# A graph kernel whose edge scores are scattered earlier, with the diagonal written by SyncE

## The reference

```
xl = (x @ Wl).reshape(n, H, D);  xr = (x @ Wr).reshape(n, H, D)      # H = 4 heads of 64
msg = xl[src] + xr[dst]
act = jnp.where(msg > 0, msg, 0.2 * msg)
e = jnp.einsum('ehd,hd->eh', act, att)       # one number per edge and head
m = segment_max(e, dst);  p = exp(e - m[dst]);  alpha = p / denom[dst]
```

## Time and profile before

| | |
|---|---|
| median of 3 runs (lowest to highest) | 3180.23 us (3179.59 to 3190.14) |
| the profiled execution: time, span | 3187.83 us, 3186.1 us |
| busy: TensorE, VectorE, ScalarE, GpSimd | 87%, 51%, 30%, 25% of the span |
| TensorE clock granted, mean | 0.906 of full speed |
| front, count | 0 to 93 us, 93 to 370 us |
| mix 0, output 0 | 370 to 934 us, 934 to 1076 us |

### The profile page before, as it was taken

How to read it: one execution, slowest core, us unless ns; L and a number is a source line. 1 busy time by engine, 2 the same in 40 slices (tenths; PEclk the granted TensorE clock), 3 DMA queues, 4 the chain that set the end, 5 groups by cost and what they waited for, 6 DMA issues and landing times. The chain is left out here.

```text
span 3186.1 us, 52553 instructions
## 1 busy us (share of the span) xinstructions
PE 2769.6 (87%) x19788; PEld 2590.7 (81%) x19788; DVE 1615.7 (51%) x3224; ACT 963.7 (30%) x1941; POOL 791.7 (25%) x780
## 2 busy tenths in 40 slices
PE   6577798988879699879997999899999989999478
PEld 6344587877879699778886999899999989999367
DVE  7466455555566288665555222245454432226455
ACT  4355322322231155314443000034333220001043
POOL 0456555554654133212210000000000001000144
PEclk9788798888889799859998999999999999999589
DMA  8733322323236698227765211111111662124174
GB/s 244 251 84 98 92 77 78 80 83 86 59 122 179 155 229 213 94 71 199 207 178 125 79 44 44 56 30 54 31 57 54 184 163 86 60 68 135 27 239 141
DMA packets 206775, 363.00 MB, mean 114 GB/s; under 512 B 38358, under 2 KB 139950, under 8 KB 205299
## 3 DMA queue, kind: packets, MB, share of 16 engines
q1 hardware_dynamic: 170117, 278.93, 30.2%
q0 software_dynamic: 36432, 80.98, 10.1%
HBM read 272.99 MB, written 98.18 MB: 116 GB/s over the span
## 5 line engine op out<-in xcount | busy, mean ns | idle before, releaser
L180 PE MATMUL mix_bank<-mix_wkv_hi,layer_act_hi 128*125 128x256 f32 x1280 | 368.2, 288 | 12.4 <-issue 12.0
L182 PE MATMUL mix_bank<-mix_wkv_hi,layer_act_lo 128*125 128x256 f32 x1280 | 366.5, 286 | 12.4 <-issue 12.1
L181 PE MATMUL mix_bank<-mix_wkv_lo,layer_act_hi 128*125 128x256 f32 x1280 | 366.7, 286 | 10.9 <-issue 10.3
L3084 POOL TENSOR_TENSOR sage_add<-sage_add,sage_bias 125x256 f32<-125x256 f32 x40 | 29.6, 742 | 1205.5 <-DMA sage_add<-resid 1205.5
L180 PEld LDWEIGHTS mix_bank<-mix_wkv_hi,layer_act_hi 128*125 128x125 f32 x1280 | 244.0, 191 | 22.2 <-issue 21.9
L567 POOL DMA_INDIRECT scored_ring<-xl,edge_idx x168 | 171.6, 1021 | 348.3 <-DVE edge_e L651 218.7
L181 PEld LDWEIGHTS mix_bank<-mix_wkv_lo,layer_act_hi 128*125 128x125 f32 x1280 | 244.5, 191 | 13.7 <-issue 13.2
L182 PEld LDWEIGHTS mix_bank<-mix_wkv_hi,layer_act_lo 128*125 128x125 f32 x1280 | 244.2, 191 | 12.9 <-issue 12.7
L924 PE MATMUL count_pa<-count_hot_s,count_hot_d 125*125 125x416 bf16 (+1 forms) x624 | 156.3, 417 | 68.2 <-DVE count_hot_s L834 36.0
L574 POOL DMA_INDIRECT scores<-edge_e,edge_idx x168 | 174.4, 1038 | 133.2 <-DMA scores<-edge_e,edge_idx 86.3
L924 PEld LDWEIGHTS count_pa<-count_hot_s,count_hot_d 125*125 125x125 bf16 x624 | 101.6, 169 | 123.2 <-DVE count_hot_s L834 49.0
(11 more groups left out here) (596 smaller groups left out, 8325.5 us busy)
## 6 DMA issues: line engine op xcount, KB each, us to landing
ffn_raw<-in_L_ffn_w_dram SPq DMA_DIRECT2D x16, 2048.0 KB
scores<-targets_hole SPq DMA_DIRECT2D x40, 546.9 KB
ffn_raw<-in_L_ffn_W_dram SPq DMA_DIRECT2D x16, 1024.0 KB
gat_sc<-scores SPq DMA_DIRECT2D x6, 2187.5 KB
mix_raw<-in_L_mix_w_qkv_dram SPq DMA_DIRECT2D x24, 512.0 KB
scored_ring<-scores SPq DMA_DIRECT2D x4, 2187.5 KB
layer_slab<-in_L_gnn_W_neigh_dram SPq DMA_DIRECT2D x7, 1024.0 KB
layer_slab<-in_L_gnn_W_self_dram SPq DMA_DIRECT2D x7, 1024.0 KB
```

The lines of the kernel that those rows point to most:

```text
L180: pe.matmul(out, lhs[0], rhs[0], start=first, stop=False)
L181: pe.matmul(out, lhs[0], rhs[1], start=False, stop=False)
L182: return pe.matmul(out, lhs[1], rhs[0], start=False, stop=last)
L3084: pool.tensor_tensor(add[:, u % 2, :], add[:, u % 2, :], bb[:, g * SLAB:(g + 1) * SLAB], ALU.add) \
```

## The change

The lag is 2 batches from the first scatter to the last; SyncE writes the diagonal, right behind its last fill, under a semaphore of its own; GpSimd's first scatter waits for that. In count the first turn is followed by 4 steps in place of 2 and the last by 1 in place of 3. In output 0 one step stands ahead of the first remainder in place of two, the next ones ahead of k = 2, 4, 6 in place of 1, 4, 7, and the last ones come later (the last in tile 7 of slab 2, not in tile 1). The number of gathers, scatters and steps is the same.

```
-LAG = 8
-CATCH = 6
+BEHIND = 2
+AT_ONCE = 2
...
     def scatter(self, pool, b, j):
...
-        pool.wait_ge(self.s_sc, 16 * (T + 1) + 16 * k)
+        if k == 0:
+            pool.wait_ge(self.s_diag, 16 * (T + 1))
+        else:
+            pool.wait_ge(self.s_sc, 16 * k)
...
-    def diagonal(self, pool):
-        pool.wait_ge(self.fill.s_fill, self.fill.count)
+    def diagonal(self, sp):
+        sp.wait_ge(self.fill.s_fill, self.fill.count)
...
     def gpsimd(self, pool, first, end):
...
         for b in range(first, end):
-            done = range(self.written(b - 1) if b else 0, self.written(b))
-            if 0 in done:
-                self.diagonal(pool)
             for j in range(EB):
                 if b + AHEAD < BATCHES:
                     self.gather(pool, b + AHEAD, j)
-                for d in done[:1]:
-                    self.scatter(pool, d, j)
-            for d in done[1:]:
-                for j in range(EB):
-                    self.scatter(pool, d, j)
+                if b >= BEHIND:
+                    self.scatter(pool, b - BEHIND, j)
...
                 counts.fill.issue(sp, len(counts.fill.left))
+                edges.diagonal(sp)
...
-                    while todo.u < COUNT_BATCHES * (t + 1) // T:
+                    while todo.u < min(COUNT_BATCHES, AT_ONCE + COUNT_BATCHES * (t + 1) // T):
...
-                for _ in range(2):
-                    if todo is not None:
-                        todo.step()
+                if todo is not None:
+                    todo.step()
                 for k in range(KD):
-                    if todo is not None and k in (1, 4, 7):
+                    if todo is not None and k in (2, 4, 6):
...
-                        if todo is not None and i in ((5, 9), (1, 4, 6, 9), (1, 4, 6, 9), (2, 5, 8))[g] and todo.left():
+                        if todo is not None and i in ((5, 9), (1, 4, 7), (1, 4, 7), ())[g] and todo.left():
```

More of the change, by code:

```diff
@@ L526, in __init__ @@
         self.s_idx, self.s_att, self.s_cell = ph.sem("idx"), ph.sem("att"), ph.sem("cell")
-        self.s_e, self.s_sc = ph.sem("e"), ph.sem("sc")
+        self.s_e, self.s_sc, self.s_diag = ph.sem("e"), ph.sem("sc"), ph.sem("diag")
         self.s_g, self.s_link = ph.sems("g", RING), ph.sem("link")
@@ L581, in diagonal @@
             n = min(R, N - 1 - t * R)
[L582 to L587, removed]
+            sp.dma_start(diag[t * R:t * R + n, 0:HEADS], self.loops[0:n, t, :]).then_inc(self.s_diag, 16)
+        sp.dma_start(self.scores[N * N - 1:N * N, :], self.loops[R - 1:R, T - 1, :]).then_inc(self.s_diag, 16)
     def landed(self, eng):
-        eng.wait_ge(self.s_sc, 16 * (T + 1) + 16 * ET)
+        eng.wait_ge(self.s_sc, 16 * ET)
     def gpsimd(self, pool, first, end):
@@ L604, in gpsimd @@
                     self.gather(pool, b + AHEAD, j)
-                for d in done[:1]:
-                    self.scatter(pool, d, j)
-            for d in done[1:]:
-                for j in range(EB):
-                    self.scatter(pool, d, j)
+                if b >= BEHIND:
+                    self.scatter(pool, b - BEHIND, j)
         if end == BATCHES:
-            for d in range(self.written(end - 1), end):
+            for d in range(end - BEHIND, end):
                 for j in range(EB):
```

## The result

The changed kernel takes 3227.4 us (median of 4 runs, 3215 to 3245) against 3180.6 (median of 4) before. By the medians it is 47 us slower, and outside the range of 3167 to 3195. The profiled execution took 3244.7 us, 17 above its median, so its rows overstate the loss a little (span 3243.0 against 3186.1: +56.9).

The account below looks back on a forecast made before the run. Bounds: VectorE-TensorE ring in count, TensorE slowed by late instructions in mix 0, VectorE's first remainder at output 0's start. Terms +3.0 + 4 - 5 - 0.8 = +1.2 us on 3187.8 gave 3189.0, median 3181.4; range 3167 to 3195.

Parts of the forecast that it names:

- Twelve scatters more in count: Count stage, turns 2 and 3: the extra early scatters lengthen turns by +4 us, between 0 and 11.4.
- the long burst stalls the counting loops: Rival, turns 2 and 3: GpSimd issuing without pause from 157 to 215 us costs +13.6, 3194 us; chance 0.15.
- Nobody waits: Count: gathers of batches 7 and 8 held behind GpSimd's waiting scatter delay nobody; VectorE needs batch 8 after turn 2; cost 0.
- Two steps more after turn 0: Count, before turn 1: two more VectorE steps of 2.26 us each cost +1.3 to +4.5 us, taken as +3.0.
- Mix 0: -5: Mix 0: fewer GpSimd issues, in catch-up batches and the first 25 us, save 5 us; bounds -1.5 to -10.
- Instructions come late while requests are under way: Mix 0: TensorE's slabs take 70.7 us against 49.85 in mix 1 because instructions arrive late during GpSimd's gathers and scatters.
- Two steps fewer after turn 9: End of count: VectorE's work ends earlier, but the stage ends with SyncE's store, so 0.
- the diagonal on SyncE: Count: SyncE issues the diagonal by 155 us, ahead of its store at 159.84; cost 0.
- the last scatters: End of output 0: 14 gaps of 4.0 us end at 1065.2, before the last store at 1074.35; cost 0.
- Output 0: -0.8: Output 0, first slab: remainder ends 2.26 us earlier, TensorE waits 1.3 for the seventh; gain 0.8, bounds 0 to -2.3.
- turn 1 after 146: Count: turn 1's first one-hot tile was expected at 142 to 145 us; after 146 would mean late gathers.
- turns 2 and 3 above 27 and 25: Count: turns of 24 and 20 us would mean no burst price; 27 and 25 would point to the burst rival.

## Why the prediction was wrong

- *Twelve scatters more in count: +4, at most 11.4.* This step failed. The mechanism is the one of the rival "the long burst stalls the counting loops", in its place (turns 2 and 3), to which I gave 0.15. The early scatters alone lengthen these turns by 11.2 us in one profile; that this is nearly the rival's 11.4 is luck, for with the moved output steps beside them (which cost nothing by themselves) it is 16, and with the count steps 28 and 31 (two profiles of the changed kernel). The price had been taken from turn 4 of before, and a turn that lies almost wholly beside requests has no row in that trace, so the nearest row was no upper bound. As a whole the early scatters cost 29.5 us, so about 18 lie outside these turns; the profiles point to mix 0, and their cause is open. "Nobody waits" for the gathers behind the diagonal was true for their data and false for what their issue does to the others.
- *Two steps more after turn 0: +3.0, at most 4.5.* Also failed in its size: 1.0053, 17 us (9 to 25). Their own 4.5 us are there (turn 1 starts 6.5 later). The rest goes with the gathers that they release, 16 in a row, which no run takes away by themselves, and with the later place of the diagonal and the first scatters. I had counted what the steps issue on VectorE and not what they set free on GpSimd. The two parts, 1.0093 and 1.0053, add up to 1.0146; the whole is at 1.0122 and 1.0132.
- *Mix 0: -5.* This step failed too, in its sign as far as can be told. Mix 0 was 10 us longer in the profile; between its first and last key/value unit it was 528.8 us against 525.0. One program's mix 0 on this kind was 550 and 566 us in two profiles, so a term of 5 can't be seen in a pair, but the seven profiles with the short lag are 18 us longer on average than the five with the old one. The mean price was about right: (565.6 - 421.3) / 313 requests is 0.46 each, where I had worked out 0.43. The 25 requests fewer (288 in the trace; I had counted 23 fewer) did not bring that price back: a mean price is no price of one request more or less.
- *Instructions come late while requests are under way:* right in what sets off the waits. The kernel that leaves the requests out shows 52.7 us a slab against 70.7, close to the slab of mix 1, on the same kind of chip. That it is the supply of instructions which is late is inferred from waits with no name; no row shows it.
- *Two steps fewer after turn 9, the diagonal on SyncE, the last scatters: 0 each.* Right here: 1.0013 for the diagonal; the last scatter was issued at 1117.1, 14 us before the last store. The two steps fewer were never run by themselves. On the quick kind SyncE waits for the scatters in output 0, and the early scatters bring 16 us there.
- *Output 0: -0.8.* The first slab gained 2.0 us (36.3 from the first memset to its seventh block's end against 38.3), with a wait of 0.89 where 1.3 was forecast. (The last remainder behind four steps comes to 972.84 - 2.26 = 970.6 and not 970.8, which brings the forecast to about 1.1.) All moved output steps together: 1.0007, nothing that can be told.
- The signs named beforehand served: turn 1 after 146 and turns 2 and 3 above 27 and 25 both came true, and the latter spoke for the rival. The former had been named as a sign of late gathers; the profile shows no wait for a gather there.

## What to carry to other kernels

Before a queue of indirect requests is moved or let run ahead, ask what the other engines do beside it: where engines already stand without a named wait, an unbroken run of requests can stop them altogether (on the slow kind of chip here), and the longest run in the profile of before is no bound for a longer one. Count what a moved instruction sets free on other queues, not only what it issues. And where a loss rests on such lateness, measure on more than one chip before the order of a kernel is tuned to it.

## What was not expected of the hardware

- The same program takes 3007 us on two chips and 3172 to 3194 on four others. The difference, 170 us, is that of leaving out 480 indirect requests on the slow kind (3004 us). On the quick kind mix 0 runs beside them at 52.8 us a slab with a granted clock of 0.99; on the slow kind at 68 to 74 (541.4 / 8 and 588.8 / 8) with 0.87 to 0.91. Why chips differ so was not found; no row shows the fetch of an instruction, and the DMA engines are at 0.27 to 0.41.
- On the slow kind 16 us of requests (13 on GpSimd) left TensorE with no matmul at all and ScalarE idle for 13 us, though neither uses their data. Reads of 128 x 16 bytes in place of the scatters lengthen the turns as much as writes (turn 2 to 35.6 us with reads, 30.9 with writes).
- On the quick kind GpSimd's indirect requests go at 1.40 to 1.46 us each over a whole stage (busy near 1.0, a gap of 0.3, and at times a wait for the scatter before), and 42 of them in a slab of 52.8 us are too many.
- Still open: why the kernel that closes the lag in mix 0 is slower (1.0065), why mix 0 is longer with the short lag, which is where some 18 us of the early scatters' price seem to lie, and what the changed kernel does as a whole on the quick kind. No kernel that computes everything was shown to be faster than before on the slow kind; on the quick kind the early scatters without any moved step are (0.9946).
